# SyncE's program up to the layers in straight lines, and the first pass's one-hots with their iota in a PSUM bank, in a four-layer graph network kernel

## What is computed

```python
h = relu(layernorm(x))
x = x + L0(h)   # features of each edge's source, scaled by its weight, one dense layer, relu,
                # MAX over the edges of a destination, concatenated with h, dense, relu
h = relu(layernorm(x))
x = x + L1(h)   # four times: h @ W, sum over edges with 1/sqrt(deg) on both sides,
                # a norm over the whole graph, relu
h = relu(layernorm(x))
x = x + L2(h)   # sums of relu'd projections over the edges of a source, dense, relu
h = relu(layernorm(x))
x = x + L3(h)   # sum, max and mean of 32 edge attributes per source, two dense layers
```

## Time and profile before

| | |
|---|---|
| device time, median of 3 runs | 14810.56 us (14802.09 to 14845.96) |
| device time of the profiled execution | 14776.96 us |
| span of the profiled execution | 14775.2 us |
| PE busy | 8251.6 us (56%) |
| DVE busy | 5889.9 us (40%) |
| ACT busy | 5765.9 us (39%) |
| POOL busy | 5862.9 us (40%) |
| mean granted TensorE clock | 0.705 of full speed |

### The profile page before, as it was taken

The page is one execution under the profiler, slowest core; times in us unless marked ns, Lnnn a source line. Parts: engine busy times, 40 slices in busy tenths (PEclk is TensorE's granted clock), DMA queues, the critical chain, the costliest instruction groups (busy, mean ns, idle before and its releaser), DMA issues. The chain is left out here.

```text
span 14775.2 us, 234540 instructions
## 1 busy us (share of the span) xinstructions
PE 8251.6 (56%) x68487; PEld 5775.3 (39%) x68487; DVE 5889.9 (40%) x10294; ACT 5765.9 (39%) x8522; POOL 5862.9 (40%) x5419
## 2 busy tenths in 40 slices
PE   3333333355555554107200003539999999997799
PEld 2222222245555453005100003435655566555455
DVE  5555555344444443105211003434444443444344
ACT  1111111133333332004100002228888888885677
POOL 5887887555555555560677771020000000000000
PEclk6555555566666666556555555669999999998999
DMA  4444444222222224519200104547767677673899
GB/s 136 140 142 143 142 137 144 61 63 66 64 65 64 64 64 53 45 31 258 53 0 14 20 20 104 137 103 200 206 188 205 188 206 205 187 205 112 153 171 163
DMA packets 2836522, 1744.01 MB, mean 118 GB/s; under 512 B 1859990, under 2 KB 2689020, under 8 KB 2835924
## 3 DMA queue, kind: packets, MB, share of 16 engines
q1 hardware_dynamic: 2509508, 1305.01, 36.6%
q10 hardware_dynamic: 153360, 277.67, 5.1%
q0 software_dynamic: 173184, 154.24, 4.8%
HBM read 1065.41 MB, written 502.11 MB: 106 GB/s over the span
## 5 line engine op out<-in xcount | busy, mean ns | idle before, releaser
L1072 PE MATMUL PS<-AG,T 128*64 128x512 bf16 (+1 forms) x22064 | 2558.5, 354 | 60.2 <-DVE RT L2047 26.9
L660 POOL DMA_INDIRECT G<-node_table,IDX x1664 | 2038.4, 1225 | 600.8 <-issue 590.7
L690 POOL DMA_INDIRECT records<-RT,IDX x1664 | 1690.0, 1016 | 1358.0 <-ACT RT L1326 853.8
L2021 DVE CAST AG<-AG 128x1792 bf16<-128x1792 uint8 x1176 | 1285.8, 1094 | 2006.3 <-PE PS L1072 1572.7
L1451 ACT CAST AG<-AG 128x1792 bf16<-128x1792 uint8 x1176 | 1968.4, 1683 | 219.7 <-DMA AG<-adj 106.7
L726 POOL DMA_INDIRECT adj<-OH,EA x1664 | 1725.8, 1037 | 671.5 <-issue 576.4
L1072 PEld LDWEIGHTS PS<-AG,T 128*64 128x64 bf16 x22064 | 1232.9, 110 | 934.1 <-ACT AG L1541 51.9
L1072 PE MATMUL PS<-AG,RT 128*64 128x512 bf16 (+1 forms) x11032 | 1506.7, 353 | 0.5 <-issue 0.3
L1451 ACT CAST M<-AG 128x1792 bf16<-128x1792 uint8 x588 | 990.7, 1685 | 284.0 <-PE PS L1072 241.9
L755 POOL DMA_INDIRECT AG<-node_table,srow x28 | 32.6, 1166 | 2680.8 <-issue 2680.8
L953 PE MATMUL PS<-R 98*128 98x128 f32 x3328 | 999.5, 394 | 0.0
(11 more groups left out here) (365 smaller groups left out, 13937.2 us busy)
## 6 DMA issues: line engine op xcount, KB each, us to landing
AG<-adj SPq DMA_DIRECT2D x2940, 224.0 KB
adj<-Z ACTq DMA_DIRECT2D x105, 1568.0 KB
G<-records SPq DMA_DIRECT2D x624, 128.0 KB
M<-same_dst SPq DMA_DIRECT2D x416, 128.0 KB
fill_rows<-Z ACTq DMA_DIRECT2D x104, 512.0 KB
runs_l<-R SPq DMA_DIRECT2D x208, 256.0 KB
G<-fill_rows SPq DMA_DIRECT2D x208, 256.0 KB
runs<-R ACTq DMA_DIRECT2D x208, 256.0 KB
```

The lines of the kernel that those rows point to most:

```text
L660: pool.indirect_dma_start(G[:, i, q * D:(q + 1) * D], None, table, bass.IndirectOffsetOnAxis(ap=IDX[:, i, q:q + 1], axis=0)).then_inc(sem( ...
L690: pool.indirect_dma_start(rec, bass.IndirectOffsetOnAxis(ap=IDX[:, i, q:q + 1], axis=0), RT[:, i, q, :], None).then_inc(sem(f"scattered{i} ...
L1072: m = pe.matmul(PS[h * D:(h + 1) * D, base + c:base + c + w], stat(t), rhs[:, h * QW + c:h * QW + c + w], start=start and t == 0, stop=sto ...
L2021: dve.tensor_copy(RING[i], RAW[i]).then_inc(sem("conv_d"), 1)
```

## The change

SP's four loops before the layers become Python loops, so that every step's DMAs stand in the program with fixed addresses and fixed wait counts. All `sp.sem_inc(sem("turns"), 1)` behind waits go, also in the layers' loop, which otherwise stays as it is. In DVE's program one copy writes the iota to PSUM bank 7 as float32, and the one-hots of pass 1 read it there. The programs of POOL, PE and ACT are the same, and so are the one-hots of pass 2.

```diff
             def attr_out(d, x):
                 sp.wait_ge(sem("e_ready"), d + 1)
-                sp.sem_inc(sem("turns"), 1)
                 rows = runs_e[bass.ds(d * CE, CE), :].rearrange("(k p) d -> p k d", p=P)
...
                 for i in range(4):
                     step(0, i, "first")
-                with sp.Fori(1, NIT) as it:
+                for it in range(1, NIT):
                     for i in range(4):
                         step(it, i, "mid")
...
             attr_step(1, 1)
-            with sp.Fori(1, NCH // 2 - 1) as u:
+            for u in range(1, NCH // 2 - 1):
                 for x in range(2):
                     attr_step(u * 2 + x, x)
...
             then(dve.tensor_scalar(pen_q, pen_q, -SELF, None, ALU.mult))
 
+            iota_p = bank(7)[:, 0:P]
+            then(dve.tensor_copy(iota_p, iota_f[:, :]))
+
             def onehots(q, s, h, digits):
...
                     w = P if d % 2 else NJ
-                    t = dve.tensor_tensor(OH[:, s, d, :, 0:w], rowbc(iota_b[:, 0:w], KC),
+                    t = dve.tensor_tensor(OH[:, s, d, :, 0:w], rowbc(iota_p[:, 0:w], KC),
                                           bc(KEYS[:, d, bass.ds(q, KC)], [P, KC, w]), ALU.is_equal)
```

## The result

The changed kernel takes 14752.39 us in the median of 11 runs (14589.58 to 14866.82), before 14826.68 in as many (14802.09 to 14845.96): a ratio of 0.9935, 95% interval 0.9906 to 0.9965. The forecast was 14370, with 14180 as the low and 14620 as the high end. The ratio is that of the means, 96 us apart, and leaves out the longest of the 11 runs of the changed kernel, which counts as a slow one. The way was right; of 440 us forecast, 74 came by the medians, and runs of the changed kernel now lie 277 us apart, those of before 44.

A forecast was written before the change was run, and what follows sets the result against it. POOL's gather chain was taken to bound pass 1, a loop through SP, PE and ACT the attribute pass after `adj_out`. -330 - 110 - 20 + 20 = -440 from 14776.96 gives 14337, as a median 14370 us; range 14180 to 14620.

The forecast's parts named there:

- Reading the holds: Pass 1: DVE operations with two SBUF inputs hold POOL's gathers, 463 us over the median; one PSUM input frees them.
- 133 us of holds left: Pass 1: other two-input DVE operations would still hold gathers, about 0.26 of their 514 us, between 60 and 225 us.
- rival B: Pass 1: one-hots reading PSUM still hold POOL through their SBUF input; only SP's part gained, 14700 us; chance 0.07.
- C: Rival, pass 1: one-hots get longer and still hold gathers; 15100 us if they double; chance 0.03.
- so nothing else becomes the bound: Pass 1: at 10.6 us a chunk, DVE needs 6.9 and PE less, so neither would limit it.
- The term was -330: Pass 1: the saving expected from the iota in PSUM, 330 us, range 240 to 403.
- four signs of being wrong: Mean gather stays 1.2 us; one-hots over 0.87; steps beside `adj_out` well below 30; SP gaps of 3 on the path.
- SP, attribute pass: After `adj_out`'s end: SP's five DMAs fall from 4.0 to 2.4 us, 1.25 a pair counted; -110, bounds -40 and -140.
- SP, pass 3: Behind `adj_out`'s first quarter: SP's DMAs start sooner but DMA engines are full; -20 us, range 0 to -70.
- Steps beside `adj_out`: Attribute pass beside the adjacency scatters: steps stay at 33 us, slow without any SP loop; gain 0.
- rival A: Beside `adj_out`: SP's instructions load a shared resource, so fewer shorten steps; -100 to -350 more, about 14150 us; chance 0.12.
- Fetching, +20: SP's 2930 more instructions must be fetched; some 11 fetches of 2.7 us on its path; +20 us, 0 to +60.

The follow-up runs named there:

- e1: Kernel before with only the iota of pass 1 in PSUM, SP keeping its loops; prompt signals: 12118.52 us, ratio 0.9724.
- e9: Kernel before with only the iota of pass 1 in PSUM, run again where signals are late: 14924.21 us, ratio 1.0102.
- e7: Changed kernel plus 16 one-element POOL iotas behind each chunk's gathers in pass 1 and a wait behind each eighth adjacency scatter; late signals: 13780.34 us, ratio 0.9335.
- e10: Changed kernel with pass 1's one-hots reading the SBUF iota again, so SP's straight lines alone; late signals: 14610.17 us, ratio 0.9885.
- e2: Changed kernel with pass 1's one-hots reading the SBUF iota again, so SP's straight lines alone; prompt signals: 12425.32 us, ratio 0.9975.
- e5: Kernel before, unchanged, run for its profile where signals were late: 14754.26 us in one run, beside 14739.27 for before.
- e3: Kernel before with three one-element POOL iotas behind each of the 1664 adjacency scatters; prompt signals: 12766.53 us, ratio 1.0243.
- e11: Changed kernel plus 8 POOL iotas behind each chunk's gathers in pass 1 and a wait behind each 16th adjacency scatter; prompt signals: 12420.00 us, ratio 0.9964.
- e13: Changed kernel plus 8 POOL iotas a chunk in pass 1 and a wait behind each 16th adjacency scatter, run again; prompt signals: 12429.53 us, ratio 0.9954.
- e15: Changed kernel, unchanged, run where signals are prompt: 12133.69 us, ratio 0.9723 against the kernel before.
- e4: Kernel before with at most 8 adjacency scatters in flight or queued, by POOL waits on two semaphores; prompt signals: 12456.58 us, ratio 0.9999.
- e16: Changed kernel plus 8 POOL iotas a chunk in pass 1 and a wait behind each 16th adjacency scatter; late signals: 14239.51 us, ratio 0.9619.

## Why the prediction was off

**Reading the holds: right.** Which gathers are held and by what, that a PSUM operand frees them, 1.03 us in the mean (1.026), 133 us of holds left (1707.9 - 1664 x 0.947 = 132; that this agrees to 1 us is luck, since 0.26 was a choice between two bounds), one-hots no longer (681 ns, just below the 690 to 760 expected). The rival B (still held) and C (longer one-hots) are out.

**"so nothing else becomes the bound": this step failed.** I checked DVE's and PE's busy time against 10.6 us a chunk and stopped there. What came to bound pass 1 was how late PE's and SP's signals arrived, which is in no busy time. The trace of before showed it beside `adj_out`, and I wrote "the slow steps come without any loop on SP, with the signals between engines late; I count 0 for them", as if it belonged to that stretch. The question not asked was why pass 1, with the same kind of DMA at nearly the same pace, was free of it. The answer is the term that I was removing: 2.2 us of holds in each chunk. e1 shows that the iota saves 342 us where signals are prompt, e9 that it costs 159 where they are late, and e7 that pauses put in their place end the stalls. The term was -330 and came out at +84 in the profiled execution; since SP's half alone took 43 us off pass 1 (e10), the iota's own part is nearer +130. None of my four signs of being wrong could have shown it: they asked for the mean gather, the one-hots, the steps beside `adj_out` and SP's gaps, and all four came out as forecast. Only the end of pass 1, at 2725 instead of 2140 to 2310, did.

**SP, attribute pass: right in mechanism and size.** -110 forecast; from first to last output 1899 us before and 1786 after, -113. The way there was partly luck: the 4.0 us that I took for every step were those of each second one, and the loads got longer. It depends on the chip as well: with prompt signals the pass lies wholly beside `adj_out` and gives nothing to the end; e2's 35 us there come from pass 1.

**SP, pass 3: about right.** -20 forecast, 1049 us before and 1034 after, -15. **Steps beside `adj_out`: right,** 33.7 us in both kernels; rival A (fewer instructions of SP relieve the others) is out.

**Fetching, +20: nothing seen.** e10's -155 us are the attribute pass (-106 against e5) and pass 1 (-43 against e5), and in the attribute pass behind `adj_out` the longest gap from an output through the four loads behind it is 0.7 us (ahead of an output SP waits for ACT, and a gap could hide there). The row it was taken from was misread as well. POOL's gap of 3 us behind each 113 scatters goes by scatters, not by instructions: in e3, with three iotas behind each scatter, it still comes each 113 scatters.

```profile
6539.85 0.99 POOL L727 DMA_INDIRECT adj<-OH,EA  x1 [3.27 <-issue]
...
6709.92 1.00 POOL L727 DMA_INDIRECT adj<-OH,EA  x1 [4.01 <-issue]
```

Between these two stand 565 rows of POOL's program, where before has 226. So it can't be set against a rule on the fetching of instructions, and what it is stays open.

The sum of the stages in the profiled executions: pass 1 +84, attribute pass -113, pass 3 and what follows it up to the attribute pass about even, layers and tail -11, fill, pass 2 and the cells +17: some -25 of -440.

## What to carry to other kernels

A stall that you remove may be what lets another engine's work through. Before you count an excess as gain, look in the same trace for a stretch that already runs as the changed stage will (here: indirect DMAs with no hold), and read how the other engines fare there. And where a stage depends on how fast signals travel, measure on more than one chip: this change is worth 2.8% on one kind and between nothing and 0.7% on the other, and 16 idle operations a chunk, with a wait behind each eighth scatter, make it 6.7% there. Where signals are prompt pauses only cost: half of these lose 2.4% (e11 and e13 against e15); the full ones were not run there.

## What the runs showed of the hardware that was not expected

- The same program took 12.46 to 12.48 ms in three groups of runs and 14.74 to 14.83 ms in the four others (the measurement of the forecast among them), alike within a group. The unheld gathers (0.94 to 0.95 us) are the same on both kinds, and so, within 2%, is all behind the attribute pass and `adj_out` (4.88 ms in e4, 4.95 before). What differs beside `adj_out` is how soon PE's and SP's results are seen while POOL issues indirect DMAs. The largest single difference, though, is pass 2, 3024 us against 2131 (e4), and its cause is open.
- Beside scatters without a pause PE advances, on average, by about one instruction for each scatter. In the changed kernel, between the start of the attribute pass's outputs and the end of `adj_out`, and in pass 3 before, beside the first part of `adj_out`:

```profile
8025.00:9035.00 1010.00, 92.31 (x360) 68.51 (x360) 73.53 (x60) 36.14 (x91) 747.43 (x729) 0.50 0.11 20
...
6090.00:6620.00 530.00, 48.49 (x198) 38.19 (x196) 30.89 (x24) 30.53 (x48) 399.72 (x395) 0.50 0.15 31
```

  360 / 12 = 30 steps, each of 12 loads and 12 matmuls, and 729 / 30 = 24.3 scatters a step; in the second row 394 instructions of PE stand beside 395 scatters. It is the seeing of the results that is late, not the work: in the kernel before, PE runs one step's 12 matmuls in 3 us, and ACT's copy of the last eight starts 10.6 us behind them.

```profile
7977.41 1.11 PE L812 MATMUL PS<-ident,RT 128*128 128x128 f32 x4 [37.38 <-DMA RT<-same_src]
...
7978.32 1.91 PE L822 MATMUL PS<-ident,G 128*128 128x128 f32 x8
...
7990.80 0.40 ACT L1242 COPY RT<-PS 128x288 f32<-128x288 f32 x1 [32.62 <-issue]
```

  What the shared way is, the traces don't say.
- On chips with late signals, pass 1 has 24 loads and 24 matmuls a chunk and 8 gathers. Beside the issue gaps it had 2.2 us of holds in a chunk (before), 2.0 (e10), 1.1 us of iotas and 0.7 of holds (e7), all without stalls, and it stalled with 0.5 and 0.5 (e16) and with 0.6 of holds (the changed kernel): so what it needs lies between 1.1 and 1.8 us a chunk, as far as chips 14 and 4 can be compared. How a pause works was only argued, not shown.
- SP's straight lines made pass 1 some 43 to 59 us shorter by themselves, on both kinds of chip (e10: gathers 1198 ns in the mean instead of 1223; e2 1198, e4 1235), by fewer or shorter holds. The cause was not tried.
